# Intra-chunk blocks of a selective scan: two heads of one chunk stacked on the partition halves, x times dt formed by channel, inner products left in PSUM

## What is computed

```python
zxbcdt = u @ in_proj_w.T                       # z0, x0, z, xBC, dt
dt = softplus(dt + dt_bias)                    # one number per token and head
xconv = silu(causal_conv4(xBC)); xs, Bm, Cm = split(xconv)   # 64, 32, 32 channels
xh = xs.reshape(B, L, 4, 16); A = -exp(A_log)  # 4 heads of 16 channels
for t in range(L):                             # the state is 16 x 32 per head
    h = h * exp(dt_t * A) + dt_t * x_t * B_t
    y_t = h . C_t
y = (y + D * xh) * silu(z)
y = y * rsqrt(mean(y * y) + eps) * norm_w
out = concat(silu(z0) * x0, y) @ out_proj_w.T
out = out * sigmoid(se2(relu(se1(mean(out)))))
```

## Time and profile before

| what | us |
|---|---|
| median of 3 runs | 72.57 |
| lowest and highest run | 72.35, 73.35 |
| the profiled execution | 72.53 |
| its span, first to last instruction | 70.7 |

### The profile page before, as it was taken

How to read it: one execution, slowest core, us unless ns; L and a number is a source line. 1 busy time by engine, 2 the same in 40 slices (tenths; PEclk the granted TensorE clock), 3 DMA queues, 4 the chain that set the end, 5 groups by cost and what they waited for, 6 DMA issues and landing times.

```text
span 70.7 us, 2413 instructions
## 1 busy us (share of the span) xinstructions
PE 59.8 (85%) x1014; PEld 39.3 (56%) x1016; DVE 51.7 (73%) x143; ACT 30.4 (43%) x71; POOL 27.8 (39%) x63
## 2 busy tenths in 40 slices
PE   2999989999969999969089999999989789695910
PEld 1335449664963337951079993994866734293700
DVE  1073286885839998999999939997438589999740
ACT  0260785824289157360628001216593700687100
POOL 5997489305774005107999881000006005000000
PEclk9999999999999999999996555999999999999999
DMA  0999700000000000000000000000000000000034
GB/s 0 289 226 348 289 14 0 9 0 0 0 0 14 0 0 0 0 9 0 0 0 9 5 0 9 0 9 5 0 0 0 9 0 0 0 0 0 9 136 161
DMA packets 1869, 2.74 MB, mean 39 GB/s; under 512 B 193, under 2 KB 1217, under 8 KB 1858
## 3 DMA queue, kind: packets, MB, share of 16 engines
q1 hardware_dynamic: 1280, 1.57, 7.1%
q10 hardware_dynamic: 578, 1.02, 4.1%
HBM read 2.06 MB, written 0.52 MB: 37 GB/s over the span
## 4 chain that ended last, share of the span: by engine, by line
PE 27%; DVE 20%; issue 4%; POOLq 2%; ACT 1%; DVEq 1%; ACTq 0%
PE ps L487 6%; PE ps L511 4%; PE ps L502 4%; PE ps L521 3%; DVE x2b L917 2%; PE ps L538 2%; PE ps L606 2%; DVE ell L883 2%; POOLq L84 2%; PE ps L529 1%; DVE qc L1071 1%; DVE xdz L907 1%; DVE qb L1073 1%; DVE h L1074 1%; DVE h L1055 1%
## 5 line engine op out<-in xcount | busy, mean ns | idle before, releaser
L290 PE MATMUL ps<-zbf 128*128 128x512 bf16 x39 | 12.0, 463 | 1.6 <-DVE zbf L805 1.3
L883 DVE TENSOR_TENSOR_SCAN ell<-ps,delta 128x512 f32<-128x512 f32 x8 | 9.2, 1206 | 0.9 <-PE ps L385 0.9
L290 PEld LDWEIGHTS ps<-zbf 128*128 128x128 bf16 x41 | 4.3, 115 | 7.8 <-issue 4.2
L606 PE MATMUL ps<-h,wk 64*64 64x256 bf16 x144 | 4.7, 274 | 1.6 <-DVE h L1074 0.9
L606 PEld LDWEIGHTS ps<-h,wk 64*64 64x64 bf16 x144 | 3.9, 106 | 2.6 <-issue 2.3
L930 DVE TENSOR_TENSOR mm<-ell,gsb 128x1024 f32<-128x1024 f32 x4 | 4.7, 1210 | 0.0
L487 PEld LDWEIGHTS ps<-mm,xdz 64*32 64x32 f32 x256 | 4.2, 133 | 0.9 <-issue 0.8
L487 PE MATMUL ps<-mm,xdz 64*32 64x64 f32 x256 | 4.6, 268 | 0.0
L337 PE MATMUL ps<-u,wtap 64*64 64x512 f32 x32 | 4.4, 614 | 0.0
L385 PEld LDWEIGHTS ps<-rows,sel 96*128 96x128 bf16 x32 | 2.0, 97 | 4.2 <-DVE ell L883 2.6
L1194 POOL TENSOR_TENSOR sc<-sc 128x1 f32<-128x1 f32 x1 | 0.2, 190 | 10.3 <-ACT sc L743 10.3
(11 more groups left out here) (247 smaller groups left out, 144.0 us busy)
## 6 DMA issues: line engine op xcount, KB each, us to landing
w1n<-c1n_in ACTq DMA_DIRECT2D x1, 288.0 KB, 5.7
w2t<-c2t_in SPq DMA_DIRECT2D x1, 288.0 KB, 6.3
w1t<-c1t_in SPq DMA_DIRECT2D x1, 288.0 KB, 7.1
x_sb<-x_in SPq DMA_DIRECT2D x1, 256.0 KB, 3.2
x_sb<-x_in ACTq DMA_DIRECT2D x1, 256.0 KB, 3.4
out<-o_sb SPq DMA_DIRECT2D x1, 256.0 KB, 2.5
out<-o_sb SPq DMA_DIRECT2D x2, 128.0 KB, 2.0
cs<-cst_in ACTq DMA_DIRECT2D x1, 240.0 KB, 6.7
```

The costliest lines, as they stand in the source:

```text
L290: mul(ps[:, bank, :], zbf[:, 0:P], zbf[:, :], start=True, stop=True)
L606: last = mul(ps[col:col + CH, CONV[turn] + far, 0:TOK], wk[row:row + CH, tap, :], src[row:row + CH, b, dy:dy + SIDE, dx:dx + SIDE], start= ...
L883: vec_.tensor_tensor_scan(dst, ps[:, SPREAD[g % 2], :], delta[:, :], 0.0, ALU.mult, ALU.add).then_inc(scanned, 1)
```

## The change

- **PE, new:** channel_steps(j), twice: four matmuls each of the widened dt (dtv) by the identity, so that dt stands by channel. **ACT, new:** a copy of each to dtc.
- **GpSimd, new:** dtv (dt widened to 16 columns), bc2 (B of each chunk written twice, 1024 elements), and xd = xc * dtc, two products of 512 elements. x_to_tokens now turns xd, so x comes to the tokens already multiplied by dt. DVE loses dl1, dl23 and the xdz products.
- **ACT, new:** eight copies of 64 x 256 from XTB to xdz. It loses the two gsb copies.
- **Inner products:** bc2 makes the weights 128 columns wide, so the result for one chunk stands on both partition halves. It stays in PSUM (GB has four banks now, two shared with others), and blocks reads it there. The selection matrix is permuted to match, so that ell has one head on each half.
- **inside:** K is 128 and holds two heads; 32 matmuls a j instead of 64. y1 is read from one bank.
- **Order:** on PE the gate z comes before the inner products and the gate x0 after the state matmuls; j = 1 of the inner products comes before j = 0, with a wait for w_copy 3 between them. The matmul for the second weight statistic goes from before L502 to between the two j of inside. Four warm-up matmuls are put in front of gated_share(0), and two are taken out before squares(1). On DVE all four blocks come before the gate products.

```diff
-        LXB, SPREAD, GB, ZB, XTB, BTB = (5, 6), (5, 6), (2, 3), (2, 3), (0, 1), 4
-        HB, YI, YA, SSQ, RB, PO = 4, (5, 6), ((0, 1), (2, 3)), (0, 2), ((1, 3), (0, 2)), (4, 7, 5, 6)
-        SE, OSUM, CONV = (0, 1), (1, 3), (2, 5)
+        LXB, SPREAD, ZB, XTB, BTB, DTC = (5, 6), (5, 6), (2, 3), (0, 1), 4, 7
+        GB, X0B, NORM, HB, YI, YA = ((2, 3), (4, 7)), (5, 6), 3, 0, (1, 2), (3, 4)
+        SSQ, RB, PO = (1, 2), ((3, 1), (4, 2)), (7, 0, 5, 6)
+        SE, OSUM, CONV = (4, 1), (2, 3), (2, 5)
...
+            def channel_steps(j):
+
+                for t in range(4):
+                    at = HEADS * (8 * j + 2 * t)
+                    last = mul(ps[:, DTC, P * t:P * t + P], dtv[:, at:at + 8, :].rearrange("p i d -> p (i d)"), ident, start=True, stop=True)
+                last.then_inc(dtc_ready, 1)
+
+            pe.wait_ge(w_copy, 1)
+            pe.wait_ge(dtv_ready, 1)
+            channel_steps(0)
...
+            def inner_products(j, p):
+
+                for k in range(2):
+                    for c2 in range(2):
+                        for b in range(2):
+                            s = slice(64 * p + 32 * b, 64 * p + 32 * b + 32)
+                            c = 2 * k + c2
+                            col = CHUNK * (4 * k + 2 * p + c2)
+                            last = mul(ps[:, GB[j][b], col:col + CHUNK], bc2[s, j, c, :, :].rearrange("n e t -> n (e t)"),
+                                       csilu[s, j, CHUNK * c:CHUNK * c + CHUNK], start=True, stop=True, tile_position=(s.start, 0))
                 last.then_inc(g_half if p == 0 else g_ready, 1)
...
+            pe.wait_ge(dtc_sb, 1)
+            channel_steps(1)
             pe.wait_ge(b_silu, 1)
             pe.wait_ge(c_silu, 1)
             pe.wait_ge(ld_wb, 16)
...
+            gate(ZB, wa_sb[:, A_Z:A_Z + CH], z_proj)
+            pe.wait_ge(bt_sb, 1)
+            pe.wait_ge(dtc_sb, 2)
+            pe.wait_ge(bc2_ready, 1)
+            inner_products(1, 0)
+            pe.wait_ge(g_half, 1)
+            inner_products(1, 1)
+            pe.wait_ge(silu_z, 2)
             pe.wait_ge(w_pool, 1)
             pe.wait_ge(w_stats, 2)
-            mul(ps[:, STAT, 96:99], half_ones, sc[:, 8:11], start=True, stop=True).then_inc(w_mm, 1)
+            mul(ps[:, NORM, 96:99], half_ones, sc[:, 8:11], start=True, stop=True).then_inc(w_mm, 1)
+            pe.wait_ge(w_copy, 3)
+            inner_products(0, 0)
+            pe.wait_ge(g_half, 2)
+            inner_products(0, 1)
             pe.wait_ge(x2_ready, 6)
+            pe.wait_ge(xd_ready, 4)
...
+                for k in range(2):
+                    for c2 in range(2):
+                        for p in range(2):
+                            for r in range(2):
+                                q0 = 64 * p + 32 * r
+                                col = TOK * b + P * k + CHUNK * c2
+                                last = mul(ps[q0:q0 + 32, YA[j], col:col + CHUNK], xdz[:, tile(j, b, k, p), c2, r, :, :],
+                                           mm[:, 2 * j + b, 4 * k + 2 * p + c2, r, :], start=True, stop=True, tile_position=(0, q0))
...
+            pe.wait_ge(m_ready, 2)
             inside(0, 0)
             inside(0, 1).then_inc(ya_ready, 1)
+            pe.wait_ge(w_pool, 2)
+            mul(ps[:, HB, 448:450], half_ones, sc[:, 16:18], start=True, stop=True).then_inc(w_mm, 1)
+            pe.wait_ge(m_ready, 4)
+            inside(1, 0)
+            inside(1, 1).then_inc(ya_ready, 1)
             pe.wait_ge(gated0, 4)
             pe.wait_ge(w_copy, 4)
+            keep_warm(4, PO[0])
             gated_share(0)
...
+            pe.wait_ge(yd_ready, 2)
             squares(0)
-            pe.wait_ge(ydx_ready, 2)
             gated_share(1)
-            keep_warm(2, YA[0][1])
             squares(1)
...
+            act.wait_ge(zero_xdz, 1)
+            for j in range(2):
+                act.wait_ge(x2_ready, 3 * j + 3)
+                for c2 in range(2):
+                    for e in range(2):
+                        heads = ps[half(c2), XTB[j], :].rearrange("s (i r e d) -> s i r e d", r=2, e=2, d=HDIM)
+                        go(xdz[half(e), 8 * j:8 * j + 8, c2, :, e, :], heads[:, :, :, e, :], ACT.Copy).then_inc(xd_ready, 1)
+            act.wait_ge(w_mm, 3)
+            go(sc[:, 12:15], ps[:, NORM, 96:99], ACT.Copy).then_inc(w_copy, 1)
...
+                dve.wait_ge(g_ready, 2 - j)
+                g = ps[:, GB[j][b], :].rearrange("p (m t) -> p m t", t=CHUNK).unsqueeze(2).broadcast_to([P, 8, 2, CHUNK])
+                tt(mm[:, 2 * j + b, :, :, :], ell[:, j, :, :, b, :], g, ALU.mult).then_inc(m_ready, 1)
...
+            pool.wait_ge(b_silu, 1)
+            gp.tensor_scalar(bc2[:, :, :, :, :].rearrange("n j c e t -> n (j c) e t"),
+                             bc[:, :, :].rearrange("n j (c t) -> n (j c) t", t=CHUNK).unsqueeze(2).broadcast_to([P, 8, 2, CHUNK]),
+                             1.0, 0.0, ALU.mult, ALU.add).then_inc(bc2_ready, 1)
+            for j in range(2):
+                bs = slice(2 * j, 2 * j + 2)
+                pool.wait_ge(x_silu, j + 1)
+                pool.wait_ge(dtc_sb, j + 1)
+                gp.tensor_tensor(xd[:, bs, :], xc[:, bs, :], dtc[:, bs, :], ALU.mult).then_inc(xdt_ready, 1)
```

154 lines of the change are left out of this document (50 added, 104 removed).

## The result

| what | before | after |
|---|---|---|
| median of 4 runs, us | 72.96 | 79.72 |
| lowest and highest | 72.35, 74.24 | 78.75, 80.93 |
| the profiled execution | 72.53 | 78.75 |
| its span | 70.7 | 77.0 |
| mean granted clock | 0.952 | 0.903 |

The ratio is 1.0954, interval 1.0894 to 1.1015. The forecast was 74.6 with a range to 76.3: the direction was right, the size was not.

What follows compares the result with a forecast made beforehand. Bound: DVE until 35.0, PE at half clock until 42.4, then DVE until 47.81. +1.4 - 1.5 + 3.9, less 1.27 and 0.6, made +2.0 on 72.53: 74.5, plus 0.1 for the clock; range 72.9 to 76.3.

Steps and rivals of the forecast that it cites:

- Term 1: PE ahead of the scans: two channel_steps rounds put the sixth scan at 28.7, DVE idle 1.3 us; +1.4 us.
- Term 2: DVE up to x_to_end: dl and xdz products gone, -1.5 us, through at 34.95.
- Term 3: Ahead of the block products: PE waits for a small copy behind eight xdz copies on ACT; +3.9 us.
- the upper sign of being right: Inner products (L409): 55 to 65 ns a pass would show the forecast right.
- Term 4: DVE from first block product to end of yg(1): 11.5 us, the 1.27 us wait for PE gone.
- Term 5: Tail after yg(1): -0.6 us, two warm-up matmuls taken out, everything from L521 on as before.
- POOL: GpSimd: dtv and bc2 1.04 us each, xd 1.2; std_ready at about 47 to 50; L1175's hold-up would go.
- A: Rival: PE stays slow and takes the bound, the second L521 begins 3.4 late; 75.9 us, chance 0.27.
- the main case: The whole kernel by the summed terms: 74.6 us, own range 73.9 to 75.3, chance 0.40.
- B: Rival: inner products' weight loads are hidden, 27 ns a pass; 73.0 us, chance 0.17.
- C: Rival: inner products' loads run one behind the other, 131 ns, blocks from 40.8; 76.5 us, chance 0.08.

Runs made afterwards that it cites:

- a_small_copy_first: Changed kernel with ACT's small copy of the weight statistics (raises w_copy to 3) ahead of the eight xdz copies; median 76.65 us.
- d_warm_as_before: Changed kernel with warm-up matmuls as in the kernel before: none ahead of gated_share(0), two before squares(1); 78.56 us, ratio 1.0608.
- f_blocks_1_first: Changed kernel with DVE's two block products of j = 1 ahead of those of j = 0; 80.94 us, ratio 1.1142.
- c_weights64: Changed kernel with 64 instead of 128 weight columns in each inner product, half of the products left out; single run, 78.44 us.
- b_warm_gap: Changed kernel with eleven warm-up matmuls in PE's wait for w_copy 3; 78.52 us, ratio 1.074.
- k: Changed kernel, small copy and j = 1 blocks first, old warm-ups, x0 gate between inner products, gate products between blocks, second statistics matmul earlier; 75.99 us, ratio 0.9947.
- l: k with nine more warm-up matmuls: six ahead of inner_products(0, ...), three ahead of the wait for hc; 73.43 us, ratio 1.0226.
- n: l with the state matmuls ahead of inner_products(0, ...) on PE; 74.99 us, ratio 1.0403.
- g_channel_later: Changed kernel with second channel_steps and x_to_tokens later on PE, GpSimd's weight statistics ahead of the second xd; 80.44 us, ratio 1.1074.

## Why the prediction was right in direction and wrong in size

**Term 1, right.** The sixth scan was forecast at 28.7 after 1.3 us of idle DVE; it came at 28.76 after 1.38. L384 took 1.14 and 1.16 for eight passes.

**Term 2, right.** DVE was to be through with x_to_end at 34.95 and was at 34.78.

**Term 3 is the step that failed, in two of its sizes.** The mechanism was as described: eight xdz copies, the small copy behind them, PE behind that, all of DVE's block products behind PE, and a_small_copy_first shows it. The sum was +3.9; it measured +6.1 (41.11 against 35.02). 0.6 of the difference is ACT's: I let follow-on copies overlap by 0.1, so that four take 1.2 us; the eight took 3.19 in one row, 0.40 each, and one has a mean of 378 ns, so they didn't overlap. ACT was still at the first four when DVE was through, and the small copy ended at 37.0, not 36.4. The other 1.6 us is PE's: the 32 passes took 4.01 us against the 1.9 + 0.5 of the sum. At full clock they take 2.28, 71 ns each, so my 60 was 0.4 us short (and above the 65 that I had named as the upper sign of being right). The larger part, 1.2, is the clock: its fall cost 1.7 us, and I had charged 0.5 without working it out from a row. In this execution it had fallen 2.3 us before the passes began. The early fall isn't what matters: in d_warm_as_before and f_blocks_1_first it fell at 37.4, close to where it fell before, and the passes still took 3.78 and 3.80. At half clock a pass of this kind takes 125 ns, so 32 x 2 x 60 ns = 3.8 us would have been the term.

On the Trainium skill's page "TensorE: Matmul & The Clock Gate", LDWEIGHTS: c_weights64 agrees with its rule that a load's time goes with the columns, as far as the direction goes (1.43 us with 64 columns, 2.28 with 128). No run varies the rows. By its figure 32 loads one behind the other would be an estimated 3.4 us; 2.28 was measured at full clock in alternating row groups, so these loads didn't run one behind the other.

**Term 4, right.** 11.5 us were forecast from the first block product to the end of yg(1), and 11.57 measured; g read from PSUM cost nothing (4.61 us for four products against 3.48 for three); the 1.27 us of waiting at y1 were gone, as foreseen.

**Term 5, wrong, by 2.0 us.** I took off 0.6 and it cost 1.4. 0.8 of the 2.0 lie between the end of yg(1) and the second L536, 2.66 us instead of 2.41 less 0.6. I had taken two warm-up matmuls off and left out the four that the change puts ahead of gated_share(0): they hold squares(0), the first root and w1t's scaling, and through these ysq(1). std_ready was late too (51.8 against the forecast 47 to 50), but not what ACT waited for. The other 1.2 are the second slow stretch. "From L521 on everything is as before" was the sentence that failed. In d_warm_as_before, with the warm-ups where they were, both are gone: 1.97 us, and no second slow stretch.

2.2 + 2.0 give the 4.2 us between the forecast 74.5 and the profiled 78.75.

**POOL.** xd took 1.27 (1.2 forecast), bc2 1.05 (1.04). The estimate of 1.1 us from the Trainium skill ("GPSIMD Engine Reference", Performance versus the Vector engine) is some 13% low here. L1175's 2.35 us are now 0.29 (L1188), but L1188 ran while DVE was idle, so this trace doesn't test the forecast. b_warm_gap does:

```profile
39.61 0.19 POOL L1194 TENSOR_SCALAR sc<-sc 128x1 f32<-128x1 f32 x1
...
39.89 0.57 POOL L1195 TENSOR_TENSOR sc<-sc 128x1 f32<-128x1 f32 x1
```

Both stand beside DVE's block products (from 39.26 on) with g in PSUM. The same two instructions took 1.02 and 1.43 us before (L1179, L1180), beside block products with gsb in SBUF. That agrees with the rule of the Trainium skill ("SBUF — State Buffer", Who interferes with whom).

**The rivals.** A was right in more than the main case allowed. PE stayed slow, and for longer than A had it. In the tail the four warm-ups and the gated share held squares(0) (51.69, A's 51.0) and ACT scaled w1t behind it (until 53.71, A's 52.1). But the bound stayed with DVE, which had no gap after 41.11. My error was to treat "PE slow" and "PE takes the bound" as one case, when the slowness hits the main case's own term first. B (27 ns) and C (131 ns at full clock) are excluded by the 71 ns. C's 131 was nearly the measured pace, for another reason.

**What isn't settled.** That idle time isn't needed for the clock to fall is shown by k, whose PE was busy throughout; that thin matmuls bring it down is argued, and which property of them would do it isn't shown. Each clock stretch here is from one profiled execution, and such a stretch moves by about 3 us between executions with the same work (34.8 and 37.4). So a shift of that size can't be put down to an edit; that dense work kept the clock up through L409 in b, l and n is clearer, since its second row took 2.28 us there and more than 3 in every other profiled execution with 128 columns. Why a pass of 64 columns takes 45 ns here and took 27 in L396 is open too.

## What to carry to other kernels

When an edit puts a small copy behind a row of large ones on the same engine, look who waits for it: here 0.17 us of ACT held both PE and DVE, and the cheapest repair of the whole change was to move that one line. Price work behind a new wait at the lower clock too, from rows at that clock, and check whether work placed earlier is thin; the clock can fall while PE is busy. Count fillers (warm-up matmuls) as work: four of them ahead of gated_share(0) held a chain over two engines. They paid where PE waits anyway ahead of short work, as in the kernel before; in l and n, where PE was itself the bound, they didn't bring the time below it. And look for the wait that comes into force when an order is changed: moving the states first gained nothing, because a shared bank tied the state reads to a block product.

## What was not expected of the hardware

- ACT's copies of 64 partitions by 256 from PSUM took 0.40 us each in a row of eight (mean 378 ns), no less than the 372 ns of a 128 x 256 read the earlier trace rows. Half of the partitions saved nothing here.
- A pass of 32 rows, 128 weight columns and 64 moved columns takes 71 ns at full clock and 125 at half (2.28 and 4.01 us for 32); with 64 weight columns 45 and 71 (1.43 and 2.27, c_weights64).
- DVE and GpSimd hold each other up in both directions: on DVE, L914 on 128 x 1 took 0.13 us alone and 0.95 beside xd (g_channel_later); on GpSimd, 128 x 1 instructions took 1.02 and 1.43 us beside block products with both inputs in SBUF (before) and 0.19 and 0.57 with one in PSUM (b_warm_gap).
- The granted clock fell with PE busy for 3.97 of the last 4.04 us (k_without_later_steps). With the same PE work it fell at 34.78 for 10.24 us in one execution and at 37.36 for 6.83 us in two others; with eleven dense matmuls ahead of the wait it fell at 39.93, for 10.24 us.
